# Rotated queries and keys stored plane by plane in DRAM, so that a loaded row is one run of 8 KB, and mask rows stored beside the keys

## The reference

```python
NL, D, H, DFF = (6, 128, 16, 512)
HD = D // H
def _rope(x):
    ...
    return jnp.concatenate([x1 * cos - x2 * sin, x1 * sin + x2 * cos], axis=-1)
def _attn(q, k, v, mask):
    scores = jnp.einsum('bqhd,bkhd->bhqk', q, k) / np.float32(np.sqrt(HD))
    scores = jnp.where(mask[:, None, None, :], jnp.float32(-jnp.inf), scores)
    w = jax.nn.softmax(scores, axis=-1)
    return jnp.einsum('bhqk,bkhd->bqhd', w, v)
```

## Time and profile before

| | |
|---|---|
| median of 3 runs | 2218.05 us (2217.97 to 2221.16) |
| profiled execution | 2213.04 us |
| its span | 2211.2 us |
| PE busy | 1802.6 us (82%) |
| DVE busy | 1723.1 us (78%) |
| ACT busy | 1517.0 us (69%) |
| POOL busy | 1035.1 us (47%) |
| mean granted clock of PE | 0.906 |

### The profile page before, as it was taken

How to read it: one execution, slowest core, us unless ns; L and a number is a source line. 1 busy time by engine, 2 the same in 40 slices (tenths; PEclk the granted TensorE clock), 3 DMA queues, 4 the chain that set the end, 5 groups by cost and what they waited for, 6 DMA issues and landing times.

```text
span 2211.2 us, 40093 instructions
## 1 busy us (share of the span) xinstructions
PE 1802.6 (82%) x13138; PEld 767.3 (35%) x13138; DVE 1723.1 (78%) x4125; ACT 1517.0 (69%) x2808; POOL 1035.1 (47%) x1506
## 2 busy tenths in 40 slices
PE   4564185278999999999999999999999999999662
PEld 2332174122333333333333333333333333333231
DVE  6766111588899888998888987889988889888777
ACT  2443031156888888888888887888888888889553
POOL 2443712824454555454554554554545545444532
PEclk9766598569999999999999999999999999999785
DMA  3001122322423343423533325333244232432100
GB/s 101 1 0 38 56 86 76 85 52 69 96 66 67 88 101 79 92 59 70 108 82 83 79 55 112 86 68 88 53 106 94 71 81 68 90 86 59 30 2 20
DMA packets 153736, 155.11 MB, mean 70 GB/s; under 512 B 32247, under 2 KB 137523, under 8 KB 153523
## 3 DMA queue, kind: packets, MB, share of 16 engines
q1 hardware_dynamic: 151487, 148.34, 28.8%
q0 software_dynamic: 2048, 4.20, 0.7%
HBM read 82.15 MB, written 67.85 MB: 68 GB/s over the span
## 4 chain that ended last, share of the span: by engine, by line
PE 55%; DVE 10%; DMA 9%; POOL 6%; ACT 5%; issue 3%; SPq 2%; POOLq 0%; DVEq 0%; ACTq 0%
PE ps L1357 14%; DMA q<-scratch_queries 8%; PE ps L1310 7%; PE ps L1321 6%; DVE smax L1878 4%; PE ps L1459 4%; PE ps L1469 4%; ACT big L1586 4%; PE ps L1368 3%; PE ps L1433 2%; PE ps L600 2%; PE ps L610 2%; PE ps L1393 2%; PE ps L1344 2%; PE ps L1332 1%
## 5 line engine op out<-in xcount | busy, mean ns | idle before, releaser
L1586 ACT ACTIVATE big<-ps 128x512 f32<-128x512 f32 x1920 | 1009.6, 613 | 214.9 <-PE ps L1321 204.6
L1878 DVE TENSOR_REDUCE smax<-ps 128x1 f32<-128x512 f32 x1536 | 966.7, 684 | 175.8 <-PE ps L1310 123.3
L1357 PE MATMUL ps<-big,vaug 128*32 128x512 f32 x3072 | 430.4, 634 | 2.3 <-ACT xnT L1594 1.2
L1310 PE MATMUL ps<-k,q 49*128 49x512 bf16 x1536 | 294.7, 394 | 80.9 <-DMA q<-scratch_queries 56.1
L1321 PE MATMUL ps<-q,k 52*128 52x512 bf16 x1536 | 291.1, 392 | 9.2 <-DVE smax L1878 3.3
L1310 PEld LDWEIGHTS ps<-k,q 49*128 49x128 bf16 x1536 | 76.1, 94 | 314.4 <-DVE smax L1878 153.1
L1789 POOL CAST mparts<-smax 128x16 bf16<-128x16 f32 x96 | 19.2, 200 | 324.4 <-DVE smax L1878 324.4
L1886 DVE TENSOR_REDUCE maxima<-ps 128x4 f32<-128x308 f32 x384 | 157.2, 469 | 9.4 <-PE ps L1344 5.9
L1321 PEld LDWEIGHTS ps<-q,k 52*128 52x128 bf16 x1536 | 78.9, 94 | 215.5 <-issue 65.4
L1775 POOL TENSOR_TENSOR rot<-rot,cs 128x512 f32<-128x512 f32 x72 | 92.0, 1277 | 103.3 <-DVE rot L1897 103.3
L1780 POOL TENSOR_TENSOR hat<-rot,rparts 128x512 f32<-128x512 f32 x72 | 82.6, 1161 | 70.6 <-ACT rparts L1634 70.6
(11 more groups left out here) (312 smaller groups left out, 2938.2 us busy)
## 6 DMA issues: line engine op xcount, KB each, us to landing
k<-scratch_keys SPq DMA_DIRECT2D x48, 384.0 KB
q<-scratch_queries SPq DMA_DIRECT2D x48, 384.0 KB, 8.1
cq<-scratch_cross_queries SPq DMA_DIRECT2D x48, 384.0 KB, 6.0
scratch_keys<-rparts SPq DMA_DIRECT2D x24, 384.0 KB, 2.5
scratch_queries<-rparts SPq DMA_DIRECT2D x24, 384.0 KB
scratch_cross_queries<-rparts SPq DMA_DIRECT2D x24, 384.0 KB
scratch_keys<-rparts SPq DMA_DIRECT2D x24, 256.0 KB, 2.2
scratch_queries<-rparts SPq DMA_DIRECT2D x24, 256.0 KB
```

Of the source, the lines that this page charges most:

```text
L1310: last = nc.tensor.matmul(out[u], m.q6[rows, v % 2, 2 * g + pr, qt * P:(qt + 1) * P], m.k6[rows, v % 2, 2 * g + pr, :], start=True, stop=True)
L1357: last = nc.tensor.matmul(m.ps[32 * j:32 * j + 32, pv_bank, :], of_head(m.vaug, v % 2 * TB + kt, g, j), of_quad("self", q)[:, j, :], start ...
L1586: nc.scalar.activation(of_quad(kind, p // 2)[:, p % 2 * 2 + u, :], bank("exp" if kind == "self" else "cross exp", p, u), ACT.Exp, scale=sc ...
L1878: nc.vector.tensor_reduce(m.smax[:, n % 2, qt, u, pr:pr + 1], bank("max", i, u), AX.X, ALU.max).then_inc(s_read["self"], 1)
```

## The change

In DRAM the layout becomes [batch][product][128 features][512 tokens] (for keys a seventh plane, `PRODUCTS + 1`, that is written once at the start with mask rows and the constant shift rows). The 128 features are put in another order (`features`): the weight columns and the rotary tables are permuted on the host, so that the feature index reads (head of the pair, feature, pair). Then a loaded row, one product and one feature of all 8 pairs, is one run of 8 KB. The six products by eight features are two dimensions with a step of 64 K elements between products, so the source of a load is [6][8][4096] elements for queries and [7][8][4096] for keys (56 rows, `ROWS_STORED`, with the mask, shift and unused rows), where it was [48][8][512]. The mask DMAs are gone. Keys and queries are loaded by one step, `load_rows`, which first waits for both stores, and both share one semaphore. `PIECES` is 1: one load step per visit. Stores write 1 KB per product where they wrote runs of 3, 2 and 1 KB (queries). The context keys get a padded layout: four times as many stores (12 for 3), and loads of 48 rows of 2 KB.

```diff
-    sp.dma_start(dst[:, 0:3, :], parts[:, 0:3, :]).then_inc(stored, 16)
-    sp.dma_start(dst[:, 3:5, :], parts[:, 0:2, :]).then_inc(stored, 16)
-    sp.dma_start(dst[:, 5:6, :], parts[:, 0:1, :]).then_inc(stored, 16)
+    for lo, hi in ((0, 3), (3, 5), (5, 6)):
+        sp.dma_start(planes(dst, lo, hi), parts[:, 0:hi - lo, :]).then_inc(stored, 16)
...
+def rows_of(src, u, first=0, last=PAIRS):
+
+    return src[:, u * ROW_BLOCK:(u + 1) * ROW_BLOCK].rearrange("c (r i) n -> c r i n", r=HD)[:, :, first:last].rearrange("c r i n -> c r (i n)")
...
-OTHER_HALF = [lane ^ (HD // 2) for lane in range(32)]
+OTHER_HALF = [lane ^ PAIRS for lane in range(32)]
+PIECES = 1
+PIECE = PAIRS // PIECES
...
-    "SP load queries": (-32643,),
-    "SP load keys": (-32960,),
+    "SP load rows": (-32643,),
...
             def store_context(n):
                 sp.wait_ge(x_lo["context"], n + 1)
                 if n:
                     sp.wait_ge(kc_loaded, 16 * 2 * B * n)
-                store_query_parts(sp, a["ctx_keys"], parts_of("context", n), x_stored["context"])
+                for b in range(B):
+                    store_query_parts(sp, a["ctx_keys"][b][:, :, 0:N_CTX], parts_of("context", n)[:, :, b * N_CTX:(b + 1) * N_CTX],
+                                      x_stored["context"])
...
-            def load_queries(v):
-                b, i = v % B, v % 2
+            def load_rows(j):
+                v, k, b, i = j // PIECES, j % PIECES, j // PIECES % B, j // PIECES % 2
+                if k == 0:
+                    sp.wait_ge(x_stored["query"], 48 * (v + 1))
+                    sp.wait_ge(x_stored["key"], 48 * (v + 1))
                 if v >= 2:
-                    sp.wait_ge(scores["self"], PER_VISIT * (v - 1))
+                    sp.wait_ge(scores["self"], PER_VISIT * (v - 2) + PER_VISIT // PIECES * (k + 1))
+                lo, hi = k * PIECE, (k + 1) * PIECE
                 for u in range(2):
-                    lo = u * ROW_BLOCK
-                    sp.dma_start(m.k6[lo + ROW_MASK:lo + ROW_SHIFT, i],
-                                 a["neg_mask"][b:b + 1, :].unsqueeze(1).to_broadcast([1, PAIRS, S])).then_inc(k_loaded[i], 16)
-                sp.wait_ge(x_stored["query"], 48 * (v + 1))
-                src = a["queries"][b].rearrange("(i u r) c n -> u (r c) i n", u=2, r=HD)
-                for u in range(2):
-                    sp.dma_start(m.q6[u * ROW_BLOCK:u * ROW_BLOCK + ROW_MASK, i], src[u]).then_inc(q_loaded[i], 16)
...
+                    at = u * ROW_BLOCK
+                    sp.dma_start(m.k6[at:at + ROWS_STORED, i, lo:hi].rearrange("p i n -> p (i n)"),
+                                 rows_of(a["keys"][b], u, lo, hi)).then_inc(loaded[i][k], 16)
+                    sp.dma_start(m.q6[at:at + ROW_MASK, i, lo:hi].rearrange("p i n -> p (i n)"),
+                                 rows_of(a["queries"][b], u, lo, hi)).then_inc(loaded[i][k], 16)
...
                 for u in range(2):
-                    sp.dma_start(m.cq[u * ROW_BLOCK:u * ROW_BLOCK + ROW_MASK], src[u]).then_inc(c_loaded, 16)
+                    sp.dma_start(m.cq[u * ROW_BLOCK:u * ROW_BLOCK + ROW_MASK].rearrange("p i n -> p (i n)"),
+                                 rows_of(a["cross_queries"][v % B], u)).then_inc(c_loaded, 16)
...
-SCRATCH = {"sent": ((SLOTS + TOP_K * T * P, D), F32), "answers": ((SLOTS, D), F32), "neg_mask": ((B, S), BF16), "neg_cmask": ((B, N_CTX), BF16), "queries": ((B, P, PRODUCTS, S), BF16),
-           "keys": ((B, P, PRODUCTS, S), BF16), "cross_queries": ((B, P, PRODUCTS, S), BF16), "ctx_keys": ((P, PRODUCTS, NC_ALL), BF16)}
+SCRATCH = {"sent": ((SLOTS + TOP_K * T * P, D), F32), "answers": ((SLOTS, D), F32), "neg_cmask": ((B, N_CTX), BF16), "queries": ((B, PRODUCTS, P, S), BF16),
+           "keys": ((B, PRODUCTS + 1, P, S), BF16), "cross_queries": ((B, PRODUCTS, P, S), BF16), "ctx_keys": ((B, PRODUCTS, P, P), BF16)}
```

More of the change, by code:

```diff
@@ L54 @@
 ROWS_ALL = ROW_SHIFT + 3
+ROWS_STORED = HD * (PRODUCTS + 1)
 SECTION_GROUPS = {"next": ("n1", "q", "k", "v"), "self": ("so", "n2", "cq"), "context": ("ck", "cv"),
@@ L292, in _ @@
             sp.wait_ge(cleared, 16 * 5)
-            sp.dma_start(a["neg_mask"], m.negmask[:]).then_inc(neg_out, 16)
+            for b in range(B):
+                sp.dma_start(a["ctx_keys"][b].rearrange("c p n -> p c n"), m.kc6[:, 0, 0:PRODUCTS]).then_inc(neg_out, 16)
             sp.dma_start(a["neg_cmask"], m.negcmask[:]).then_inc(neg_out, 16)
-            sp.wait_ge(neg_out, 32)
+            for u in range(2):
+                for first, last in ((0, PAIRS), (4 * PAIRS, ROW_BLOCK)):
+                    sp.dma_start(a["keys"][:, PRODUCTS, u * ROW_BLOCK + first:u * ROW_BLOCK + last],
+                                 m.negmask[:].unsqueeze(1).to_broadcast([B, last - first, S])).then_inc(shift_out, 16)
+                for b in range(B):
+                    sp.dma_start(a["keys"][b, PRODUCTS, u * ROW_BLOCK + PAIRS:u * ROW_BLOCK + 4 * PAIRS].rearrange("(r i) n -> r i n", i=PAIRS),
+                                 m.shift_rows[:]).then_inc(shift_out, 16)
+            sp.wait_ge(neg_out, 16 * (B + 1))
             for u in range(2):
                 shift, mask = u * ROW_BLOCK + ROW_SHIFT, u * ROW_BLOCK + ROW_MASK
-                for i in range(2):
-                    sp.dma_start(m.k6[shift:shift + 3, i], m.shift_rows[:]).then_inc(shift_out, 16)
                 for b in range(B):
@@ L781 @@
         "first query", "less query", "second query", "third query", "product key", "rope key", "rotate key", "first key", "less key",
-        "second key", "third key", "store query", "store key 0", "store key 1", "store key 2", "load queries", "load keys", "values",
+        "second key", "third key", "store query", "store key 0", "store key 1", "store key 2", "load rows", "values",
         "copy values", "weights next", "gain next"),
@@ L1022, in layers @@
     w_sem = sems("weights", SECTION_GROUPS)
-    q_loaded, k_loaded, m_rows = [sems(n, range(2)) for n in ("queries_loaded", "keys_loaded", "shift_rows")]
+    m_rows = sems("shift_rows", range(2))
+    loaded = [sems(f"rows_loaded{i}_", range(PIECES)) for i in range(2)]
     c_loaded, kc_loaded, c_m_rows = sem("cross_queries_loaded"), sem("context_keys_loaded"), sem("cross_shift_rows")
@@ L1159, in store_queries @@
                 if i >= B:
-                    sp.wait_ge(q_loaded[i % 2], 32 * ((i - B) // 2 + 1))
+                    for k in range(PIECES):
+                        sp.wait_ge(loaded[i % 2][k], 64 * ((i - B) // 2 + 1))
                 store_query_parts(sp, a["queries"][i % B], parts_of("query", i), x_stored["query"])
@@ L1172, in store_stage @@
                     if kind == "key":
-                        sp.wait_ge(k_loaded[i % 2], 64 * ((i - B) // 2 + 1))
+                        for k in range(PIECES):
+                            sp.wait_ge(loaded[i % 2][k], 64 * ((i - B) // 2 + 1))
                     else:
@@ L1266, in _ @@
                     load_cross(i)
-                for i in due("SP load queries", now):
-                    load_queries(i)
-                for i in due("SP load keys", now):
-                    load_keys(i)
+                for i in due("SP load rows", now):
+                    load_rows(i)
                 for i in due("SP load context", now):
@@ L2338, in layer_cols @@
         return np.concatenate(vecs).T
-    cos, sin = rotary_tables()
+    cos, sin = (table[turned] for table in rotary_tables())
     got = {
```

40 lines of the change are left out of this document (19 added, 21 removed).

## The result

The changed kernel takes 2463.68 us (2459.17 to 2464.98) against 2218.01 us before: ratio 1.1106, 95% interval 1.1082 to 1.1131. It is 11% slower. The forecast was 2463 us, so the total fits to 1 us. The terms that made it up fit less well; the part on the prediction goes through them.

The account below looks back on a forecast made before the run. PE holds most of the chain, the queries' load 8% of the span, with PE standing still 56.1 us; 183 + 40 + 4 + 18 = +245 on 2213.0 gives 2458 us, 2463 at the median; range 2240 to 2540 us.

Parts of the forecast that it names:

- The engine count: Loads of queries and keys: after the change they run on 6 and 7 DMA engines, not 16.
- The time of a transfer: One 384 KB load transfer: 2.42 us today plus a fixed 1.55 us per load; 4.6 us after the change.
- Keys and queries: Self-attention load: 19.95 us instead of 11.25, +8.7 us in 21 visits, +183 us (bounds +36 and +288).
- the engines don't meet: Lower bound of a load transfer: each engine keeps the stores' 23.0 GB/s, 2.85 us.
- the top: Upper bound of a load transfer: each engine keeps the pace of today's loads, mean 11.2 GB/s, 5.85 us.
- Its sum of 2496 us: Whole-kernel alternative, not adopted: 2213 + 21 x 9.7 + 23 x 2.2 + 28, or 2501 us at the median.
- The stores: Stores of queries, in 1 KB pieces for 3 KB: 0.2 us in each of 21 visits, +4 us.
- The cross load and the context: Cross load 10.75 us after issue, +1.75 us in 23 visits, +40 us; context loads +3 us in 6 layers, +18 us.
- TensorE's clock: PE after waits: longer wait adds none; new cross-load wait could add 1.7 us each, in the range only.
- Mask DMAs and q<-mt: Mask DMAs of 16 KB and small q<-mt transfers around the loads: no effect on the time, 0 each.
- A: Rival for the loads: fewer engines, none in another's way, 2.85 us a transfer, 2258 us; chance 0.24.
- B: Rival for the loads: all 16 engines still serve them, 2.42 us a transfer stays, 2218 us; chance 0.11.

Follow-up runs that it names:

- merged: The changed kernel with the 128 features in another DRAM order, so a load's 48 or 56 rows are read as one dimension: 2260.82 us, ratio 1.0199.
- no_mask: The kernel before the change with the mask DMAs of visits 2 to 23 left out: 2215.7 us, ratio 0.9994.
- merged_order: merged with a visit's four loads issued as keys 0, keys 1, queries 0, queries 1: 2223.89 us, ratio 1.0018.
- pad_self: merged with 16 unused rows behind each DRAM plane of queries and keys, so self-attention loads read two dimensions again: 2370.26 us, ratio 1.0695.

## Why the prediction was right

By its own steps:

**The engine count** was the step that decided, and it held: 26 counting packets a load, and 203 of 246 us undone by merged. It was read from the q<-mt, where 3 divides 6. (The stretch of the earlier trace rows lists two q<-mt as issued, but none of their packets falls into it, so its 32 counting packets are the cross load's, as the prediction says.) The Trainium skill's rule (DMA: Bandwidth & Descriptors, section "Why a DMA increments its semaphore by 16 and not by 1") says that a DMA gets the largest number of engines up to 16 that divides the slowest dimension of both sides. The traces agree for 6 by 48, 7 by 56 and, in merged, 56 by 56 with 14.

**The time of a transfer** was set at 4.6 us, with 1.55 us fixed for a load. Both sizes were wrong, and the fault is in the reading of the earlier trace rows: its 6.0 us is the median over both transfers of a cross load, and not the time of the second. In the visit at 1293 the second is issued at 1293.6 and lands after 6.7 us, 7.1 us after the first issue; the mean over the visits is 7.4 us, not 6.4. So before the change a transfer took (11.5 - 7.4) / 2 = 2.0 us and the fixed part was 3.4 us. After it the loads of four and of two take 17.8 and 10.8 us, which gives 3.5 us a transfer and 3.8 us fixed. The pieces say the same: an engine writes 8 of them in a transfer, at 439 ns each.

**Keys and queries** were set at 19.95 us a load, +8.7 us, +183 us. Measured are 17.8 us, +6.4 us, and a wait longer by 6.8 us a visit, 143.8 us in total. The term was 39 us too large: 3.5 us a transfer for 4.6, in part made up for by the fixed part. The true value lies between "the engines don't meet" (2.85) and the top (5.85), nearer to the first than was taken. The rate per busy engine in the stretches above rises towards the end of the load: 129 / (16 x 0.45) = 17.9, 135 / (16 x 0.38) = 22.2 and 97 / (16 x 0.25) = 24.3 GB/s, while fewer and fewer engines are busy.

The Trainium skill (SBUF — State Buffer, section "Door 1: The DMA port swizzle") says that four neighbouring partitions and those 32 above share a port. The prediction's estimate from it, 4.84 us a transfer, was too high too: measured are 3.5. With 2.0 us for a transfer of before in place of 2.42 the same estimate is 4.0. No run shows which ports the engines used. Its sum of 2496 us adds 28 us for stores and context where the prediction's own terms are 22; with those it is 2490.

**The stores** were set at 4 us. SP's wait for the last store before the loads rose from 39.8 us in 23 visits to 42.8 us in 21, 0.3 us each. That fits the half microsecond a visit by which PE's wait grew more than the load.

**The cross load and the context** were set at +40 and +18 us. The new wait is 58.9 us for both. In the 17 visits without context it is 1.9 us each (forecast 1.75); in the 6 with it, 4.5 us, so the context adds 2.7 us each, 16 us (forecast 3 us each, 18). Both terms are right. That the cross load came out at 10.8 us, forecast 10.75, is luck, since the transfer was taken 1.1 us too long twice, and the fixed part 2.3 us too short. For one context, SP issues the context loads at 1487.23 and the cross load at 1499.08, 11.85 us later; before it was 8.76: 3.1 us. The 12 stores took SP 12.28 us and not 5, and were still hidden.

```profile
1467.13 12.28 SPq L769 DMA_DIRECT2D scratch_ctx_keys<-cond_rows  x12
1485.66 1.47 SPq L1243 DMA_DIRECT2D q<-mt  x2
1487.23 6.07 SPq L1236 DMA_DIRECT2D kc<-scratch_ctx_keys  x8
...
1499.08 1.48 SPq L1227 DMA_DIRECT2D cq<-scratch_cross_queries  x2
```

**TensorE's clock** was left out of the sum. This step failed: "a longer wait adds none; a new wait at the cross load could add 1.7 us each. Not in the sum, but in the range". PE was busy 48.6 us longer. In the 15 us behind the waits for queries it worked 106 us at a granted clock of 0.50, where it was 61 before, and behind the cross waits 56 us, where it was none. Half of each increase is lost: 22 and 28 us. So a longer wait did add some. The stretch in the earlier trace rows at 0.50 throughout misled: it stands behind one of the longest waits of before (3.6 us), and behind a wait of 2.2 us the first 3.6 us had 0.73.

**The order of the DMAs** had no term; the prediction only says of the queries' earlier issue that it "gains nothing, since the engines drain the same queue". The order costs 35 to 40 us with 14 to 16 engines and nothing clear of the noise with 6 or 7. It could not show in the total.

**Mask DMAs and q<-mt** at 0: no_mask agrees for the first; no run takes up the second.

Together: waits +143.8 and +58.9, busy PE +48.6, which are 251 us, and the profiled spans differ by 250.8. The forecast was +245. The terms for keys, queries and their stores were 43 us too large, the missing clock 49 us, and cross and context fit to 1 us. The 6 us that remain are hidden by the 5 us put on top for the median, since the profiled run after the change is itself at the median. So the engine count, and the waits that follow from it, were foreseen; the single microsecond is luck, and the range, not the point, is what the working had earned. Of the two rivals that stood closest, A (no meeting) needed a load of 12.95 us, and B is excluded by the packet count.

## What to carry to other kernels

Before changing a layout, write down the dimensions of both sides of the DMA as they are issued: a slow dimension of 6 or 7 takes more than half of the engines away, whatever the length of the rows, and an order of axes in which two dimensions fall into one cost nothing here (merged_order, 1.0018). Count the packets under 512 B in a stretch with one DMA: it is the number of engines. Longer rows were worth nothing here, where something else limited the rate; the rate per busy engine (GB/s by 16 times the share), half of that of the stores, told so before the work was done. And take the time of a load of two transfers from its last landing, not from a median over both.

## What the runs showed that was not expected

- With 14 to 16 engines, four loads in the order half 0, half 1, half 0, half 1 take 11.5 or 11.6 us in the mean, in the order 0, 0, 1, 1 they take 12.6 or 12.7 us, with 1 KB pieces as with 8 KB rows. That two halves loaded from two queues at once don't go faster (154 to 169 GB/s) sits badly beside this; the cause is open.
- 48-row loads run at 172 to 185 GB/s on 16 busy engines, 128-row loads of the same bytes at 261 to 273 GB/s with a share of 0.72 to 0.76.
- A new wait of about 3 us per visit in front of the cross maxima cost 1.1 us more of busy PE each time, at the lower granted clock. Prolonging an old wait from 2.7 to 4.1 us (before to merged) cost 0.9 us, and from 4.1 to 8.8 us (merged to pad_self) only 0.4 us.
